# The second MLP matmul of a Fourier-filter block with its weights held in the array

## The reference, cut to what matters

```python
residual = x
h = layer_norm(x, n1_g, n1_b)
h = afno_filter(h, w1, b1, w2, b2)
h = h + residual
residual = h
h = layer_norm(h, n2_g, n2_b)
h = jax.nn.gelu(h @ mw1 + mb1, approximate=False)   # 64 -> 256
h = h @ mw2 + mb2                                   # 256 -> 64
return h + residual
```

## Time and profile before

| what | value |
|---|---|
| median of three runs | 1069.26 us |
| span of the profiled execution, first to last instruction | 1067.7 us |
| the run that stands nearest to it | 1067.75 us |
| TensorE busy | 949.2 us (89%) |
| VectorE busy | 719.9 us (67%) |
| ScalarE busy | 558.1 us (52%) |
| GpSimd busy | 272.1 us (25%) |
| one loop step (from 480 to 581 us) | 101 us |
| the 32 instructions of the second MLP matmul in a slice | 3.13 us |

### The profile page before, as it was taken

One profiled execution on the slowest core, in us unless ns is written; L12 is line 12 of the kernel. 1 busy time (PEld: TensorE's weight loads), 2 busy tenths in 40 slices (PEclk: granted clock), 3 DMA queues, 4 the chain that ended last, 5 costly groups with the idle time before them and its releaser, 6 DMA issues.

```text
span 1067.7 us, 18451 instructions
## 1 busy us (share of the span) xinstructions
PE 949.2 (89%) x6263; PEld 817.9 (77%) x6263; DVE 719.9 (67%) x2061; ACT 558.1 (52%) x1139; POOL 272.1 (25%) x107
## 2 busy tenths in 40 slices
PE   6989963887999999999999999999998999799787
PEld 6976553685689768976897689768976998499465
DVE  4456786189767776777676767676886688543762
ACT  0002011763776577657765776577647753775333
POOL 2000004034422332233223322332233224230110
PEclk8985565988999999999999999999999999989889
DMA  9922002011000300030003000200000000000001
GB/s 270 261 67 61 1 0 61 1 34 28 1 19 18 83 5 17 17 85 2 17 17 84 3 17 17 87 1 17 17 27 1 19 27 19 0 27 18 18 26 36
DMA packets 9956, 40.78 MB, mean 38 GB/s; under 512 B 1232, under 2 KB 1232, under 8 KB 8208
## 3 DMA queue, kind: packets, MB, share of 16 engines
q1 hardware_dynamic: 9888, 40.00, 13.4%
HBM read 27.15 MB, written 12.85 MB: 37 GB/s over the span
## 4 chain that ended last, share of the span: by engine, by line
PE 57%; DVE 16%; ACT 14%; issue 8%; DMA 4%; DVEq 0%; SPq 0%; ACTq 0%
PE psum L1024 13%; PE psum L909 9%; PE psum L1009 7%; PE psum L962 7%; ACT p_y L1112 7%; ACT o_g L1121 4%; PE psum L943 4%; PE psum L983 4%; PE psum L897 3%; PE psum L836 3%; DMA n<-x_dram 2%; DVE o_g L285 2%; PE psum L884 2%; DVE hbuf L568 2%; DVE stats L527 2%
## 5 line engine op out<-in xcount | busy, mean ns | idle before, releaser
L1153 ACT ACTIVATE hid<-psum,hbias 128x448 f32<-128x448 f32 x224 | 136.2, 634 | 132.2 <-PE psum L1009 131.5
L1024 PEld LDWEIGHTS psum<-prm,hid 128*112 128x112 f32 x1792 | 187.1, 182 | 8.5 <-ACT hid L1153 4.6
L1024 PE MATMUL psum<-prm,hid 128*112 128x96 f32 x1792 | 191.3, 267 | 2.3 <-ACT hid L1153 2.3
L354 POOL TENSOR_TENSOR hbuf<-hbuf,prm 112x1792 f32<-112x1792 f32 x15 | 63.3, 4217 | 328.4 <-DVE hbuf L595 328.4
L644 DVE TENSOR_TENSOR n2T<-psum,n2T 64x448 fp32r<-64x448 f32 x112 | 69.7, 622 | 102.5 <-ACT n2T L1145 101.3
L382 POOL TENSOR_TENSOR p_y<-over,under 116x512 f32<-116x512 f32 x64 | 77.2, 1208 | 201.7 <-ACT under L1171 201.6
L1009 PE MATMUL psum<-n2T,mw1h 128*128 128x448 f32 x224 | 101.8, 455 | 26.4 <-DVE n2T L644 12.8
L909 PEld LDWEIGHTS psum<-cst,hbuf 112*112 112x112 f32 x512 | 99.8, 286 | 20.5 <-issue 19.6
L909 PE MATMUL psum<-cst,hbuf 112*112 112x116 f32 x512 | 99.4, 358 | 18.1 <-DVE hbuf L777 18.1
L962 PE MATMUL psum<-cst,p_y 116*128 116x224 f32 (+1 forms) x480 | 102.1, 356 | 3.0 <-POOL p_y L382 3.0
L1100 ACT COPY u_r<-psum 112x464 f32<-112x464 f32 x64 | 35.0, 547 | 119.8 <-PE psum L909 119.8
(11 more groups left out here) (115 smaller groups left out, 1713.1 us busy)
## 6 DMA issues: line engine op xcount, KB each, us to landing
xin<-x_dram SPq DMA_DIRECT2D x9, 1568.0 KB, 8.9
out_dram<-oslice SPq DMA_DIRECT2D x56, 224.0 KB, 2.2
ybuf<-x_dram SPq DMA_DIRECT2D x2, 1568.0 KB, 18.9
fbuf<-x_dram SPq DMA_DIRECT2D x2, 1568.0 KB, 22.4
n<-x_dram SPq DMA_DIRECT2D x2, 1568.0 KB, 25.5
xin<-x_dram SPq DMA_DIRECT2D x4, 392.0 KB, 5.3
prm<-params_dram SPq DMA_DIRECT2D x1, 771.5 KB, 26.3
cst<-consts_dram SPq DMA_DIRECT2D x1, 652.0 KB, 18.9
```

Of the source, the lines that this page charges most:

```text
L354: nc.gpsimd.tensor_tensor(h, h, row("b1", WP), ALU.add).then_inc(h_ready, 1)
L1024: last = nc.tensor.matmul(t[0:ROWS, at:at + 96], hid[:, m, w % 2, (w // 2) * ROWS:(w // 2 + 1) * ROWS], pp("mw2")[:, 128 * m + zeros:128 * ...
L1153: nc.scalar.activation(hid[:, q % 2, q // 2, :], ring_c[k % RING_C][:, 0:4 * ROWS], ACT.Gelu, bias=hbias[:, q % 2:q % 2 + 1]).then_inc(c_a ...
```

## The change

The second MLP matmul is turned around. Its weights, 64 columns of `mw2` for each half of the hidden channels, are the stationary operand; the GELU outputs, 448 columns at a time, move. The output of even image columns (v = 0) goes to PSUM partitions 0 to 63, that of odd ones to 64 to 127, which are two 64-column parts of the array. That is 4 matmuls of 448 columns (8 instructions) instead of 16 of 96. The output now has channels on the partitions, so ScalarE copies it to SBUF (`mlp_t`) with the bias `mb2` as its activation bias, and TensorE turns it back with 4 transposes (`mlp_out`), to which VectorE adds the residual as before. GpSimd's `bias_f` and its semaphore go. The chunk order gets a new entry, `out`, in the middle of the next slice; VectorE's and TensorE's orders follow.

```diff
+C_ORDER = [("n2", 0, 0)]
+for _s in range(SLICES):
+    C_ORDER += [("hid", _s, 0), ("hid", _s, 1)]
+    if _s > 0:
+        C_ORDER.append(("out", _s - 1, 0))
+    C_ORDER += [("hid", _s, 2), ("hid", _s, 3)]
+    if _s < SLICES - 1:
+        C_ORDER.append(("n2", _s + 1, 0))
+    C_ORDER.append(("mlp", _s, 0))
+C_ORDER.append(("out", SLICES - 1, 0))
...
+    what, s, q = C_ORDER[k]
+    return {"n2": ("dve", lo_done(s)), "hid": ("act", gelu_done(s, q)),
+            "mlp": ("act", turned_done(s)), "out": ("dve", out_done(s))}[what]
...
-                def bias_f(i):
...
-                    if s == 0:
-
-                        dve.wait_ge(f_biased, i + 1)
...
-                    def slice_(s, before, after):
-
+                    def slice_(s, first_part, before, after):
+
+                        first_part()
+                        if behind and s > 0:
+                            ev_mlp(i - 1, s - 1)
                         before()
                         if behind and s < SLICES - 1:
                             ev_rest(i - 1, s + 1)
                         after()
-                        if behind:
-                            ev_mlp(i - 1, s)
...
                             last.then_inc(pe_c, 1)
+                        if v == 0 and s > 0:
+                            mlp_out(i, s - 1)
                     fill(2)
                     if s < SLICES - 1:
                         transpose_n(i, s + 1)
                     fill(3)
...
+                    t = free_c(i, C_AT["mlp", s, 0])
+
+                    pe.wait_ge(c_act, i * C_ACT + gelu_done(s, 3))
+                    for m in range(2):
+                        for v in range(2):
+                            last = nc.tensor.matmul(t[C * v:C * v + C, 0:4 * ROWS], pp("mw2")[:, C * m:C * m + C],
+                                                    hid[:, m, v, :], start=(m == 0), stop=(m == 1))
+                    last.then_inc(pe_c, 1)
+
+                def mlp_out(i, s):
+
+                    t = free_c(i, C_AT["out", s, 0])
+                    pe.wait_ge(c_act, i * C_ACT + turned_done(s))
+                    for w in range(SW // 2):
+                        last = nc.tensor.transpose(t[0:ROWS, w * 128:w * 128 + 128],
+                                                   mlp_t[:, s % 2, w * ROWS:(w + 1) * ROWS], ident)
                     last.then_inc(pe_c, 1)
...
-                    for k in range(4, 8):
+                    for k in range(4, 6):
+                        inv_h(i, k)
+                    if behind:
+                        mlp_out(i - 1, SLICES - 1)
+                    for k in range(6, 8):
                         inv_h(i, k)
...
                     fill(3)
+                    k = C_AT["mlp", s, 0]
+                    act.wait_ge(pe_c, i * C_CHUNKS + k + 1)
+                    nc.scalar.activation(mlp_t[:, s % 2, :], ring_c[k % RING_C][:, 0:4 * ROWS], ACT.Identity,
+                                         bias=pp("mb2")).then_inc(c_act, 1)
```

More of the change, by code:

```diff
@@ L638, in ev_rest @@
                 def ev_rest(i, s):
-                    k = 0 if s == 0 else 5 + 6 * (s - 1)
+                    k = C_AT["n2", s, 0]
                     dve.wait_ge(pe_c, i * C_CHUNKS + k + 1)
@@ L649, in ev_mlp @@
                 def ev_mlp(i, s):
-                    k = 6 + 6 * s if s < SLICES - 1 else C_CHUNKS - 1
+                    k = C_AT["out", s, 0]
                     dve.wait_ge(pe_c, i * C_CHUNKS + k + 1)
-                    if s == 0:
-                        dve.wait_ge(f_biased, i + 1)
-                    if s == 3 and last_pair(i):
-                        dve.wait_ge(f_biased, i + 2)
                     uses = 4 if s % 2 == 0 else 3
@@ L1006, in mlp @@
                                 fill(v)
-                            t = free_c(i, 1 + 6 * s + 2 * v + m)
+                            t = free_c(i, C_AT["hid", s, 2 * v + m])
                             for wt, p in ((mw1h, 0), (mw1l, 1)):
@@ L1015, in mlp @@
                     fill(3)
-                    k = 6 + 6 * s if s < SLICES - 1 else C_CHUNKS - 1
-                    t = free_c(i, k)
-                    pe.wait_ge(c_act, i * C_ACT + 4 * s + 4)
-                    for w in range(SW):
-                        at, zeros = (w * C, 32) if w < SW - 1 else (w * C - 32, 0)
-                        for m in range(2):
-                            last = nc.tensor.matmul(t[0:ROWS, at:at + 96],
-                                                    hid[:, m, w % 2, (w // 2) * ROWS:(w // 2 + 1) * ROWS],
-                                                    pp("mw2")[:, 128 * m + zeros:128 * m + zeros + 96],
-                                                    start=(w == 0 and m == 0), stop=(w == SW - 1 and m == 1),
-                                                    skip_group_check=True)
+                    t = free_c(i, C_AT["mlp", s, 0])
[11 more added lines that the diff above has]
+                                                   mlp_t[:, s % 2, w * ROWS:(w + 1) * ROWS], ident)
                     last.then_inc(pe_c, 1)
@@ L1150, in gelu @@
                     for q in range(4):
-                        k = 1 + 6 * s + q
+                        k = C_AT["hid", s, q]
                         act.wait_ge(pe_c, i * C_CHUNKS + k + 1)
@@ L1322, in layout @@
     put("mw1", np.tile(i["L1_conv_mw1"], (2, 1)))
-    m = np.zeros((HH, 2, 128), np.float32)
-    m[:, :, 32:32 + C] = i["L1_conv_mw2"].reshape(2, HH, C).transpose(1, 0, 2)
-    put("mw2", m)
+    put("mw2", i["L1_conv_mw2"].reshape(2, HH, C).transpose(1, 0, 2))
     put("beta", rows(i["L0_conv_beta"]))
@@ L1328, in layout @@
     put("b1", rows(i["L1_conv_n1_b"]))
-    put("mb2", rows(i["L1_conv_mb2"]))
     fb2 = i["L1_conv_b2"].reshape(2, 2, CH).transpose(1, 0, 2)
```

48 lines of the change are left out of this document (25 added, 23 removed).

## The result

The changed kernel takes 1085.3 us (median of 4, 1080.77 to 1090.1); the kernel before, run beside it, 1069.54 (median of 4, 1067.75 to 1071.48). The ratio is 1.0145, 95% interval 1.0112 to 1.0179: slower by 1.5%. The profiled execution of after is the longest of its four, 1090.1 us with a span of 1088.3. Part of that is no matter of the change: its first MLP matmul starts at 302.56 instead of 296.20, behind input loads that took 28.9 us instead of 25.5.

A forecast was written before the change was run, and what follows sets the result against it. TensorE, busy 89%, looked like the bound, with ScalarE as near the limit in slices 1 and 2 and VectorE nearly unbroken in 5 and 6. +3.6 - 1.0 - 0.5 = +2.1 us gave 1071; own range 1062 to 1080, with rivals 1058 to 1105.

The forecast's parts named there:

- in program order, five steps, M = 1.89: New matmul's block in each slice: instructions start in program order, parts 0 0 1 1 0 0 1 1, five steps of 0.377 us.
- rival 2: New matmul: the two array parts overlap wholly, M = 1.51 us, no layout cost; 1061 us. Chance 0.08.
- The layout: Change of array layout before and after the block: 0.17 us a slice, between a floor of 0 and 0.34.
- Rival 1: The upper rival, on the new matmul: parts do not overlap, M = 3.02 us; +34 us, 1103. Chance 0.30.
- The gate: With `out` between them, hid 2 waits for GELU 1, not GELU 0: hid 1 to hid 2 at least 1.37 us.
- The walk: One loop step followed slice by slice, new hid 0 starts against old: even at +0.1 us before layout costs.
- Slice 5: Loop step: slice 5 starts at +0.3; VectorE's full queue carries +1.6 us through slices 5 and 6; step ends +0.1.
- GpSimd's bias goes; 0: GpSimd's removed bias, 54.3 us in all: no engine in a loop step waits for its additions, so 0 gained.
- The sum: Whole kernel: +0.6 us a step, +3.6 for six steps, -1.0 and -0.5 for the rest; +2.1 in all.
- Step 7: Last step, no layer norm beside it, slice 0's block at the low clock: -1.0 us, an estimate.
- The tail: Slices after the loop: 0.8 us shorter for slices 0, 1, 3, 4, 5, less later waits and end; -0.5 us together.
- Rival 3: Overlap as forecast, gate at hid 2 free because ScalarE catches up: 0.80 us a slice, 1069 - 45 = 1024. Chance 0.07.

The follow-up runs named there:

- v_outer: The changed kernel with the new matmul's loops swapped, all four instructions of column part 0 before the four of part 1: 1085.2 us (one run).
- one_part: The changed kernel with both halves of the new matmul sent to the same 64-column part of the array: 1127.7 us (one run; before 1068.7).
- short_bias_h: The changed kernel with GpSimd's addition of the first layer norm's bias cut from 28 image columns to 1 per half: 1074.3 us (one run).
- gate_only: The kernel before with one wait more, hid 2 also waiting for GELU 1 in slices 1 to 6: 1121.4 us against 1067.0 (one run each).

## Why the prediction was right or wrong

- **Sign and size.** The likeliest time was 1071 and the kernel takes 1085.3. That is inside 1058 to 1105, and on the side that had 0.53, but outside the forecast's own range of 1062 to 1080. What held it in the wide range was the upper rival, and the cause is not that rival's.
- **The block.** The step "in program order, five steps, M = 1.89" is wrong. v_outer shows that the parts don't wait for each other's place in the program, and M is 1.50 with 0.15 around it: rival 2's M. The "up to 2x" of the Trainium skill ("TensorEngine Tiling (Array Packing)", Theoretical Speedup), which it states for a dimension of at most 64, agrees: 3.15 us on one part, 1.65 on two. What I gave as evidence, that matmuls start in program order throughout, came from rows in which every matmul used the whole width of the array. They could not show it.
- **The layout.** I took 0.17 us a slice; the slot holds 0.15 beside its four steps and some 0.1 lies ahead. Together with M, I said 2.06 and it is about 1.75. This error speaks for the change.
- **Rival 1, no overlap.** one_part is that kernel, at 1127.7. The rival's step was +4.1 above the forecast, and measured it is +4.5 above after. Its time of 1103 was 25 too low, and 14 of these are the miss that it shares with the forecast.
- **The gate.** Right as a mechanism and in its first size. In slice 1 hid 1 starts at 530.18 and hid 2 at 531.66: 1.48, said 1.40. In slice 2 it is 2.48 (540.28 to 542.76), since ScalarE's fills lie between GELU 0 and GELU 1. The walk gave slices 0 to 4 -0.93, +0.56, +0.89, +0.18 and -0.4; measured are -0.93, +0.87, +1.04, +0.16 and -0.46. That the block is 0.3 shorter than said does nothing in slices 1 and 2, as ScalarE sets their end.
- **Slice 5 is the step that failed.** The prediction gave slices 5 and 6 together -0.2; they came to +2.02, and two runs with the collision taken out are 2.1 us shorter in slice 5. I moved VectorE's queue back by 1.6 us, all of it because of L644, and asked what is behind it on VectorE and on TensorE. I did not ask what the delayed norm of slice 4 releases on GpSimd, nor what runs on VectorE at that moment. That the addition of `out` waits 2.19 us ahead of that norm is not in the text at all. "GpSimd's bias goes; 0" looked at the addition that is removed; the one that stays was the one to look at.
- **The sum.** A step was said to be +0.6. Steps 2 to 5 are +2.86 each, step 1 is +4.0 and step 6 +2.0: 17.4 us where 3.6 was said. Step 7 was -1.0, and is -0.9. The tail was -0.5 and is -2.3. 13.8 + 0.1 - 1.8 = 12.1, and with the 2.1 that was said this is the 14.3 of the account but for rounding. Why step 1 differs from the next four stays open.
- **The tail.** Slices of 6.22 us were said; those from 1058.55, 1065.09 and 1071.24 are 6.54, 6.15 and 6.07. Slices 1 and 2 were to cost 1.7 together and cost 1.5. What came better is slice 0: 6.80 us instead of 8.48, where 0.8 was said. In before its block took 3.96 us there at a granted clock of 0.78, in after 1.72 at 1.00. The price in its slice 2 is there as described, the norm behind an addition that waits for `out`:

```profile
1049.69 0.69 DVE L661 TENSOR_TENSOR oslice<-psum,fbuf 112x512 f32<-112x512 f32 x1 [2.29 <-PE psum L1035]
...
1054.42 1.01 PE L999 MATMUL psum<-cst,n 112*128 112x112 f32 x4 [2.88 <-DVE n L580]
1055.36 3.25 PE L1026 MATMUL psum<-hid,prm 128*64 128x448 f32 x8
```

- **Rival 3, a gate that costs nothing.** It had 1024 and 0.07. With the gate moved and the readers' order moved with it the kernel takes 1041. So the simple subtraction fails even then, in slices 1 and 2, which the walk had put down to ScalarE.
- **What stays open.** With the collision out (short_bias_h) the step is 0.8 above before, where +0.6 was said. That is near in part by luck: the block was put 0.3 us a slice too long, and slices 1 and 2 came out 0.5 us worse together than the walk had them. That kernel's slices are 0.9, 0.2, 0.2, 1.0, 1.5, 0.2 and 1.5 us shorter than those of gate_only. So the cheaper block pays where TensorE sets the end of the slice and hardly at all in slices 1, 2 and 5. In 1 and 2 ScalarE's queue is the likely reason, which is argued from the traces. What else holds slice 5 no run separates.

## What to carry to other kernels

When a result goes through a second pass (bank, copy, transposes), look first at its reader's place in the in-order queues. Move the producer and the reader together: moving the producer alone cost here another 1.2 to 2.9 us a step, and moving both turned +1.5% into -2.3%. For each operation that comes later, follow what it releases, on every engine, to the instruction that it will then meet; look at the additions that stay, not only at those that go. A gain on TensorE arrives only in the slices whose end TensorE sets, and not where another engine's queue does, so sum it over those slices, not over all.

## What the runs showed of the hardware

- Float32 matmuls of 448 columns on two 64-column parts of the array run wholly beside each other: eight in 1.65 us, against 3.15 on one part. The order in the program didn't matter, even with all four of one part ahead of the other's (1.66).
- VectorE's subtraction of 112x1792 takes 2.03 us alone and 4.04 beside GpSimd's addition of 4.01 us, met after 1.85 us of it. Met for only its last 0.36 us, it took 2.25.
- After 1.70 us in which TensorE was busy for 0.07, the granted clock was 0.61 in the next 2.78 us and 0.73 in the 2.25 behind; the block took 2.31 us instead of 1.72. In the tail TensorE stood idle for 2.96 us (1044.58 to 1047.54); from 1048.91 the granted clock was 0.58 for 2.63 us, then 0.50, and the block at 1055.36 took 3.25.
